# A metaformer block on one Trainium2 core: rows centred once, a 31-row replication, a four-bank ring

## The reference, cut to what matters

```python
def _L0_conv_ref(Z_raw, ...):
    z = _layernorm(Z_raw, ln1_w, ln1_b)
    g = jax.nn.sigmoid(z @ gate_w.T + gate_b)
    proj = (z @ lrp_w.T + lrp_b) * Z_mask_row[..., None] * g
    left, right = jnp.split(proj, 2, axis=-1)
    tri = jnp.einsum('bikc,bjkc->bijc', left, right)
    go = jax.nn.sigmoid(tri @ og_w.T + og_b)
    z2 = _layernorm(tri, ln2_w, ln2_b) @ op_w.T
    return tri + go * (z2 + out_bias)

def _L0_ffn_ref(x, router_w, router_b, expert_w, expert_b):   # E = 8 experts, K = 2
    router_probs = jax.nn.softmax(x @ router_w + router_b, axis=-1)
    top_p, top_i = jax.lax.top_k(router_probs, K)
    top_p = top_p / jnp.sum(top_p, axis=-1, keepdims=True)
    expert_out = jnp.einsum('bnd,edc->bnec', x, expert_w) + expert_b
    gathered = jnp.take_along_axis(expert_out, top_i[..., None], axis=2)
    return jnp.einsum('bnk,bnkc->bnc', top_p, gathered)

x = x + _L0_conv_ref(_ln_c(x), ...)      # x is (1, 128, 128, 32)
t = _to_tokens(x)
t = t + _L0_ffn_ref(_ln_t(t), ...)       # layer norm over the 32 channels, eps 1e-5
```

## Time and profile before

| | |
|---|---|
| median of 3 runs | 194.69 us (192.22 to 196.98) |
| the profiled execution | 194.69 us, span 192.9 us |
| granted TensorE clock, mean | 0.761 |
| PE busy (of the span) | 144.9 us (75%) |
| DVE busy | 122.0 us (63%) |
| POOL busy | 95.1 us (49%) |
| ACT busy | 80.1 us (41%) |
| DMA | 15.85 MB, mean 82 GB/s |

### The profile page before, as it was taken

The page is one execution under the profiler, slowest core; times in us unless marked ns, Lnnn a source line. Parts: engine busy times, 40 slices in busy tenths (PEclk is TensorE's granted clock), DMA queues, the critical chain, the costliest instruction groups (busy, mean ns, idle before and its releaser), DMA issues.

```text
span 192.9 us, 2124 instructions
## 1 busy us (share of the span) xinstructions
PE 144.9 (75%) x655; PEld 61.4 (32%) x655; DVE 122.0 (63%) x207; ACT 80.1 (41%) x139; POOL 95.1 (49%) x82
## 2 busy tenths in 40 slices
PE   6757429698689796579999993617866697898793
PEld 2325306566589452124333331112200021111110
DVE  1889799966442858583732168399649746626562
ACT  3438432255313499931314727327413333422410
POOL 3241999359800446706962023225835657555450
PEclk9999655579969999957999999555555558555769
DMA  5993000000000000000000789999897001101102
GB/s 156 368 433 129 0 0 0 2 0 3 0 0 2 0 0 3 0 0 0 2 0 0 164 207 203 208 209 207 201 208 191 35 23 54 56 0 54 45 12 109
DMA packets 5530, 15.85 MB, mean 82 GB/s; under 512 B 1296, under 2 KB 1296, under 8 KB 5392
## 3 DMA queue, kind: packets, MB, share of 16 engines
q1 hardware_dynamic: 5520, 15.72, 29.4%
HBM read 5.23 MB, written 2.10 MB: 38 GB/s over the span
## 4 chain that ended last, share of the span: by engine, by line
PE 55%; DVE 20%; ACT 11%; issue 5%; POOL 4%; DMA 2%; DVEq 0%; POOLq 0%
PE ps L955 14%; PE ps L944 8%; PE ps L767 5%; PE ps L815 4%; PE ps L830 4%; POOL work L377 3%; PE ps L732 3%; PE ps L785 3%; PE ps L824 3%; DVE lr L1059 2%; DVE stats L1019 2%; ACT triF L583 2%; DVE work L1309 2%; DMA xk<-in_x_k 2%; DVE work L1053 2%
## 5 line engine op out<-in xcount | busy, mean ns | idle before, releaser
L944 PE MATMUL ps<-w3F,selb 24*128 24x512 bf16 x64 | 19.1, 568 | 11.0 <-DVE prod L1309 5.4
L377 POOL TENSOR_TENSOR work<-work,late_sb 128x512 f32<-128x512 f32 x16 | 20.5, 1302 | 10.6 <-ACT work L519 10.6
L625 ACT ACTIVATE wcopy<-ps 128x512 f32<-128x512 f32 x24 | 14.3, 594 | 27.2 <-PE ps L944 25.7
L732 PE MATMUL ps<-w1m,work 64*128 64x256 f32 x128 | 20.7, 474 | 1.5 <-ACT work L496 1.5
L944 PEld LDWEIGHTS ps<-w3F,selb 24*128 24x128 bf16 x64 | 3.6, 98 | 41.4 <-issue 20.3
L405 POOL TENSOR_TENSOR work<-tri,stats 128x512 f32<-128x512 f32 x8 | 8.2, 1048 | 16.9 <-DVE stats L1144 16.9
L732 PEld LDWEIGHTS ps<-w1m,work 64*128 64x128 f32 x128 | 14.5, 232 | 5.7 <-issue 1.5
L1059 DVE TENSOR_TENSOR lr<-ps,work 128x512 f32<-128x512 f32 x16 | 10.9, 689 | 7.5 <-POOL work L377 7.4
L421 POOL TENSOR_TENSOR xi<-xi,xk 128x512 f32<-128x512 f32 x8 | 10.1, 1264 | 10.5 <-DVE xk L1173 10.5
L717 PE MATMUL ps<-early_sb,work 128*128 128x128 f32 x32 | 7.0, 356 | 10.9 <-DVE lr L1059 9.2
L955 PE MATMUL ps<-work,wexp 128*32 128x512 f32 x64 | 14.6, 1005 | 0.0
(11 more groups left out here) (129 smaller groups left out, 293.4 us busy)
## 6 DMA issues: line engine op xcount, KB each, us to landing
lr<-triF SPq DMA_DIRECT2D x32, 128.0 KB, 2.4
xi<-in_x_F SPq DMA_DIRECT2D x1, 2048.0 KB, 12.3
tri<-triF SPq DMA_DIRECT2D x16, 128.0 KB, 2.3
xk<-triF SPq DMA_DIRECT2D x16, 128.0 KB, 2.4
out<-xi SPq DMA_DIRECT2D x8, 256.0 KB, 2.0
xk<-in_x_k SPq DMA_DIRECT2D x4, 256.0 KB, 5.3
xk<-in_x_k SPq DMA_DIRECT2D x2, 512.0 KB, 7.0
early_sb<-in_early SPq DMA_DIRECT2D x1, 513.0 KB, 5.0
```

The source lines that it names most:

```text
L377: pool.tensor_tensor(v, v, m, ALU.mult).then_inc(s_gm, 1)
L625: act.activation(wcopy[:, a * W:(a + 1) * W], ps[:, HELD + POOL_N[a] % 4, :], ACT.Copy)\
L732: m = pe.matmul(ps[:, 4 * slot + 2 * p + b, q % 2 * 2 * F1:(q % 2 + 1) * 2 * F1], fring[rows, slot * W + q * P:slot * W + (q + 1) * P], w1 ...
L944: pe.matmul(ps[:, HELD + n % 4, :], selb[rows, h * P:(h + 1) * P], col(w3F, g)[rows, :], start=True, stop=True).then_inc(s_wb, 1)
```

## The change

- **Rows centred once.** `centre_again`, `add_std` and the late `z_copy` go. `square_and_copy` squares the centred rows and copies them to `triF` straight away. The router takes its bias from a product with the deviation (`logit_bias`, 8 products of 128 x 32 on 512 columns), and the experts' matrix loses its dependence on channel 0 (`against_first`), whose row carries the bias instead.
- **The deviation in the redundant channel's row.** The replication copies rows 1 to 31 of each token, so 31 rows where there were 32; 16 more copies to a half, of 4 rows x 2 KB, put the deviation into the partitions 0, 32, 64 and 96 of the homes. They are on SyncE's queue behind the copies of the second and of the fourth pair, with one semaphore to a half (`s_xd`), for which every product waits.
- **First half's chain first.** All engines' lists of stage 3 to 5 are reordered, so that groups 0 to 3 go through update, centring, logits and selection ahead of groups 4 to 7. The residual is GpSimd's alone; VectorE copies the turned groups 1 and 3.
- **One ring of four banks** (0 to 3) for turned groups, gates, updates, centred rows, roots, variances, logits, weights and expert sums.
- Two calls of `keep_warm` with 12 products each, and one early table load on ScalarE (`load_roots`).

```diff
 for r in range(R):
     to = xrep(2 * p, r, groups=2)
     for e in range(R):
-        sp.dma_start(to[C * e:C * e + C, :], triF[C * r:C * r + C, 2 * p * W:(2 * p + 2) * W])\
-            .then_inc(s_xr[p][r], 16)
+        sp.dma_start(to[C * e + 1:C * e + C, :],
+                     triF[C * r + 1:C * r + C, 2 * p * W:(2 * p + 2) * W]).then_inc(s_xr[p][r], 16)
+if p % 2:
+    h = p // 2
+    sp.wait_ge(s_sf, h + 1)
+    for g in range(HG):
+        for r in range(R):
+            row = C * g + E * r
+            sp.dma_start(xrep(HG * h + g, r)[0:P:C, :], stdF[h][row:row + R, :]).then_inc(s_xd[h], 16)
...
     dve.wait_ge(s_xr[g // 2][token_of(n)], 16 * R)
+    dve.wait_ge(s_xd[g // HG], 16 * R * HG)
...
-def square5(g):
+def square_and_copy(g):
     act.wait_ge(s_z, g + 1)
     wait(act, s_v5, g // HG)
-    act.activation(col(ring, g % HG), ps[:, HELD + g % HG, :], ACT.Square).then_inc(s_q5, 1)
+    act.activation(col(ring, g % HG), ring_bank(("z", g)), ACT.Square).then_inc(s_q5, 1)
+    act.activation(col(triF, g), ring_bank(("z", g)), ACT.Copy).then_inc(s_zf, 1)
...
+def logit_bias(h):
+    pe.wait_ge(s_sf, h + 1)
+    for g in range(HG):
+        m = pe.matmul(ring_bank(("logit", h))[slot_rows(g), :], lcp("slot_bias")[:, C * g:C * g + C],
+                      stdF[h][:, :], start=False, stop=True)
     m.then_inc(s_l, 1)
...
+ScalarE's list: triF_copy(0) square4(0) triF_copy(2) out_gate(0) square4(1) out_gate(1) square4(2)
+square4(3) load_roots tri_std(0) triF_copy(4) root_copy(0) triF_copy(5..7) out_gate(2) out_gate(3)
+square4(4..7) square_and_copy(0) tri_std(1) square_and_copy(1) root_copy(1) square_and_copy(2)
+square_and_copy(3) x1_std(0) logit_copy(0) logit_turn_copy(0) out_gate(4..7) square_and_copy(4)
+square_and_copy(5) probabilities(0) square_and_copy(6) square_and_copy(7) x1_std(1) ...
...
+VectorE's list: ... tri_root(0) tri_scaled(0..3) gated_update(0) tri_squares(4) gated_update(1)
+tri_squares(5) gated_update(2) tri_squares(6) gated_update(3) tri_squares(7) tri_root(1)
+tri_scaled(4..7) gated_update(4) ...
```

More of the change, by code:

```diff
@@ L198, in bass_metaformer @@
         s_xr = [[sem(f"replicated{p}_{r}") for r in range(R)] for p in range(G // 2)]
+        s_xd = [sem(f"std_replicated{h}") for h in range(2)]
         s_wb = sem("weights_spread")
@@ L424, in _ @@
             pool.wait_ge(s_trd, 4)
-            for g in range(G):
+            for g in range(4):
                 centred4(g)
@@ L428, in _ @@
             residual(0)
+            residual(1)
+            for g in range(4, G):
+                centred4(g)
             residual(2)
             closed(0)
+            residual(3)
             closed(1)
-            residual(4)
             closed(2)
             closed(3)
+            residual(4)
+            residual(5)
             residual(6)
-            for g in range(4, G):
-                closed(g)
+            closed(4)
             def rank(n, at):
@@ L810, in update @@
                 pe.wait_ge(s_ts, g + 1)
[L811 to L815, removed]
+                ring_wait(pe, ("u", g))
+                pe.matmul(ring_bank(("u", g)), w4U[:, :], col(tri, g), start=True, stop=True).then_inc(s_u, 1)
             def centre_x1(g):
                 pe.wait_ge(s_x1, g + 1)
[L820 to L830, removed]
+                ring_wait(pe, ("z", g))
+                pe.matmul(ring_bank(("z", g)), centre, col(xi, g), start=True, stop=True).then_inc(s_z, 1)
             def variance(h):
@@ L903, in _ @@
             centre_x1(1)
+            turn_root(1)
+            centre_x1(2)
+            spread_root(1)
+            centre_x1(3)
+            logits(0)
+            variance(0)
             update(4)
-            centre_x1(2)
+            out_gate(4)
+            logit_bias(0)
+            turn_logits(0)
             update(5)
-            centre_x1(3)
+            turn_std(0)
+            out_gate(5)
             update(6)
-            centre_again(0, 1, 2)
+            out_gate(6)
             update(7)
[L911 to L921, removed]
+            out_gate(7)
+            for g in range(4, G):
+                centre_x1(g)
+            logits(1)
             variance(1)
-            centre_again(7)
-            add_std(1)
+            logit_bias(1)
             turn_std(1)
-            logits(1)
             turn_logits(1)
+            keep_warm(HELD, STAY_WARM)
             def used_before(numbers, n):
@@ L1212, in _ @@
             tri_scaled(3)
-            tri_root(1)
-            gated_update(0)
-            gated_update(1)
-            tri_scaled(4)
-            gated_update(2)
-            tri_scaled(5)
-            gated_update(3)
-            tri_scaled(6)
-            tri_scaled(7)
-            for g in range(HG, G):
-                gated_update(g)
-            x1_root(0)
+            gated_update(0)
+            tri_squares(4)
+            gated_update(1)
+            tri_squares(5)
+            gated_update(2)
+            tri_squares(6)
+            gated_update(3)
+            tri_squares(7)
+            tri_root(1)
+            for g in range(4, G):
+                tri_scaled(g)
+            gated_update(4)
             def of(tile, n, inner=E):
```

218 lines of the change are left out of this document (108 added, 110 removed), and 6 rows, old and new, of the table RING.

## The result

The changed kernel takes 440.23 us (median of 4 runs, 437.58 to 441.72) against 193.74 us before (192.22 to 196.98), a ratio of 2.277 with a 95% interval of 2.253 to 2.300. The profiled execution took 437.58 us with a span of 435.8; it is the shortest of the four. Executions of one kernel differ by up to 4% here, and each ratio with an interval compares undisturbed executions only, so that it need not equal the quotient of the medians.

The account below looks back on a forecast made before the run. Bound now: a chain through all engines, replication hidden with 15 us slack. After: start 89 + 312 copying + 2.5 small copies + 2 landing = 405.5, + 30.75 last groups = 436.3, + 1.79 around the span = 438 us; range 412 to 600.

Parts of the forecast that it names:

- The start of the copies: SyncE's replication starts once group 1 of triF is centred, at 89 us, 17 us earlier; bounds 86 and 105.8.
- The copy of 31 rows: In the replication, 31 being prime, one engine moves all 126,976 bytes: 4.88 us a copy, 312 us for 64.
- The rate: One engine's speed in a replication copy: 26.0 GB/s taken, between 26.5 or 22.1 (loads) and 14.1 (replication).
- The bound from the load without contention: Rate per engine in the load at 8 to 12 us, 26.5 GB/s, giving 4.79 us a replication copy.
- The two waits: Products wait for the deviation's copies queued behind the large ones: first half until 248 us, second half until 405.5.
- The end: After the last copies land, the four last groups take 30.75 us as before, at the clock's lower level.
- The range: Total time 412 to 600 us, leaving out the spread copies and the far end.
- lower case of 415 us: Low bound for one engine at about the load's rate: copies start at 86 us, at 26.5 GB/s.
- upper case of 510: High bound for one engine at about the load's rate: 22.1 GB/s and a start some us later.
- the middle case: Replication copies on one engine at 4.88 us each from 89 us on, total 438 us.
- The rival of spread copies: Replication copies still spread over engines at 0.64 us and stay hidden: 191.5 us, or 184; chance 0.15.
- the clock held: In the last stage, 12 warming products lift the clock: 5.9 us a group instead of 7.4, time 184 us.

Follow-up runs that it names:

- full rows: The changed kernel with all 32 rows copied again, the deviation's copies waiting until a half's 32 copies have landed; 199.77 us.
- 16 and 15 rows: The changed kernel with each 31-row copy cut into one of 16 rows and one of 15; 241.07 us in one run.
- one update moved: The changed kernel with 32-row copies and gated_update(4) moved behind the first half's first candidates on VectorE; 201.14 us, ratio 1.046 to the kernel before.
- the ladder: The kernel before with copies starting at row 1 and 30, 28, 27 and 25 rows in the four pairs; 195.41 us in one run.

## Why the prediction was right, point by point

- **The start of the copies.** 89 forecast, 88.6 measured, and that close a hit is in part luck. Three of the experiments run the same instructions up to there, and in their profiled executions the first copy is at 94.06 (full rows), 94.91 (16 and 15 rows) and 93.69 (one update moved). The granted clock from 80 to 85 us was 0.50 to 0.56 in them and 1.00 in the profiled execution of the changed kernel, and in the first `tri_root(0)` was already at 76.7 instead of 74.2; the forecast had no term for this. The other three executions of the changed kernel took 2.4 to 4.1 us more than the profiled one. In that one the steps held: `tri_root(0)` at 74.2 (73.5), the first `tri_scaled` at 77.4 (76.6), ScalarE's table load ahead of `tri_std(1)`, and group 1 of `triF` behind it. The first warming products took 0.23 us each (11 in 2.54), the lower of the two prices.
- **The copy of 31 rows.** One engine, 4.88 us forecast, 4.83 measured. That one engine carries it is shown by 464 and 336 closing packets where 31 rows were copied and 1424 where 32 were, and by the DMA share of a sixteenth; that it is the divisor and neither the odd count nor the start at row 1 by the ladder. The Trainium skill's rule (DMA: Bandwidth & Descriptors, "Why a DMA increments its semaphore by 16 and not by 1") takes the largest divisor up to 16, and it agrees with every count tried: 32, 31, 30, 28, 27, 25, 16, 15 and 4 rows. The estimate of 299 us for 64 copies from the port figure of the Trainium skill (SBUF — State Buffer, "Door 1: The DMA port swizzle") was 10 us low; the measured 4.83 gives 309.
- **The rate.** The bound from the load without contention (26.5 GB/s) was the right neighbour: 26.3. The replication's 14.1 GB/s an engine did not carry over to an engine that works alone. That it came from sharing the destination was argued and not tried by itself. The ladder fits it: the fewer engines a copy used, the more each busy engine moved. By its windows that is 15.7 GB/s at 15 engines (128 GB/s at a share of 0.51), 21.7 at 9 (149 at 0.43) and 23.1 at 5 (122 at 0.33).
- **The two waits.** Products of the first half at 248 forecast, 249.8 measured; those of group 4 at 405.5, measured 406.75. The last small copy is issued at 398.3 and the chain shows 8.24 us to its landing: the queue runs some copies ahead of the engine, so the backlog appears behind the last issue. The hit at 405.5 holds two misses that cancel: the copies took 3 us less than forecast, and from their end by that rate (88.6 + 309 = 397.7) to the product it is 9.0 us where I had 4.5 for the small copies and the landing. What fills the rest of the 9.0 was not separated.
- **The end.** 30.75 us from group 4 on, measured 29.05 (406.75 to 435.8), at a mean granted clock of 0.73 where the same stretch had 0.67 before. The prediction called that stretch one at the clock's lower level; at a mean of 0.67 it was only in part. What the 1.7 us come from was not separated.
- **The range.** Its lower case of 415 us does not follow from the bounds that it names: a start at 86 and 4.79 us a copy add up to 430. The upper case of 510 needs a start near 105.8 and not only some us later. The measured time lies near the middle case, so nothing turned on it.
- **The rival of spread copies was mis-sized.** Had the copies spread, I gave 191.5 us, or 184 with the clock held. The changed kernel with full rows takes 199.8. Two terms of that sum failed. I had the second half's logits 3 us earlier than before; they come 7.8 us later (132.9 against 125.13; in the changed kernel itself, at 129.89, 4.8 us later). And the warming products do not shorten the last stage: from the first product to the end it is 60.4 us there and 60.6 before, at a mean granted clock of 0.69 instead of 0.60.
- **Where the reordered lists lose.** Centring once gains about 5 us in the old order, and no effect of the warming calls shows. So the reordered lists with the ring of four banks lose about 12 us (199.8 against 188.0, or 199.6 without the warming calls on the chip of the 188.0; the deviation also travels in another way there, but no product waits for it in either). Between the two profiled executions the loss is complete when the second half's logits arrive, at 132.90 against 119.38, and the last stages are alike (60.4 and 59.8 us). The chain that ended last in the version with full rows goes through these pieces between 100 and 141 us:

```profile
107.11 1.28 ACT L594
108.41 0.70 ACT xk L594
109.20 0.76 DVE xk L1182
110.00 0.66 PE ps L856 x4
110.66 0.87 PE ps L808 x2
111.56 0.70 ACT xk L594
112.35 0.76 DVE xk L1182
...
121.37 0.75 DVE xk L1182
...
132.90 0.69 DVE pair L1243
```

L594 is ScalarE's gate, L1182 VectorE's `gated_update` and L808 TensorE's product for the next gate. The gate of group 4 stands behind the first half's logits and a table load, TensorE's products (L856, L808) wait for that group's update, and the gates of groups 5 and 6 follow one update at a time; `gated_update(7)` then stands behind the first selection. I had it at about 109.5, and it came at 121.37 (116.62 in the changed kernel), where the old order has it at 101.43. This explains why moving `gated_update(4)` alone gained nothing. It is read from the traces; whether the order or the ring accounts for more of it was not tried.

## What to carry to other kernels

Count the rows of every copy on the queue: dropping one row of 32 made 64 copies nearly eight times slower, while 30, 28, 27 or 25 rows cost nothing that the time of the one run shows. If one row has to hold something else, copy all of them and overwrite it afterwards, or put it in place before, and do not leave it out. The number of closing packets in a profile, divided by the copies, tells how many engines each one used on average.

## What the runs showed of the hardware that I had not expected

- The queue's time for one issue depends on the shape: 0.59 us for 32 rows, 0.77 for 30 and 28 rows, 0.70 for 27 and 25, 0.50 for 4 rows. It was not the bytes, as the smaller copies of 15 and 16 rows had medians of 0.69 to 0.81 in their three homes. Why is open. It made the split 19 us dearer than I had taken it.
- An issue blocks when the engine is behind: the first three 31-row issues took 0.6 to 0.7 us, the fourth 2.69, and from the fifth on they take about 4.79 us each on the queue, the time of the copy itself. 32 of them were issued in 140.3 us, which is 29 times 4.83, so about three copies were in flight.
- A higher granted clock in the last stage (a mean of 0.69 against 0.60) went with a length of 60.4 instead of 60.6 us. The banks of the sums differ between the two kernels, so this is a comparison and not a test of the clock alone.
